# Round 0 of the experts by blocks of 128 tokens, head by head, and x moved in 16 outer pieces

## The chip, the cores and the metric

One core of a Trainium2 chip runs the whole program as one kernel. Its engines are TensorE (PE, with weight loads as PEld), VectorE (DVE), ScalarE (ACT) and GpSimd (POOL); SyncE (SP) issues the DMAs. They run side by side and wait for one another through semaphores. The metric is the device time in microseconds (us) of one execution; each number below is the median of several.

## The reference

x is 16 sequences of 256 tokens with 512 features. Four steps follow one another, each added to x with a gain: a retention layer and a feed-forward layer (here: attention), a long convolution over key, value and query, and a mixture of experts. The changed stage does the last two:

```python
x = x + jnp.tanh(g_xattn[1]) * _L1_xattn_ref(ctx_2048, ctx_2048, _layernorm(x, axis=-1), L1_xattn_ssm_kernel, L1_xattn_D, 8)
x = x + jnp.tanh(g_ffn[1]) * _L1_ffn_ref(_layernorm(x, axis=-1), L1_ffn_Wg, L1_ffn_bg, L1_ffn_Wgate, L1_ffn_bgate, ...)
```

The convolution forms products of key and value, convolves them along the feature axis with a Toeplitz matrix and adds a skip term, then weighs the result with the query. The experts are a router (softmax over six), six routed experts of 256 hidden features and a shared one of 512: `silu(gate) * up`, then `down`.

## The kernel before

Three blocks of code run one after the other: `scores_block`, `attn_block` and `experts_block`. A block ends when every engine and the DMAs it waits for are done. All orders are written out by hand, one list of calls for each engine; a list is executed strictly in order, and each call first waits on its semaphores.

**Attention to experts.** `attn_block` works on 8 chunks (NCH) of 512 tokens, each of 4 blocks (TJ) of 128. `store` (L708) writes each finished block of x to DRAM. `fetch_x` and `copy_x` (L693 to L706) bring the rows that round 0 of the experts needs into SBUF ahead of time; copy_x takes rows of the last chunk straight from SBUF. SP's last instruction of the block waits for all these DMAs (`early_in`).

**Which tokens a round has.** `experts_block` also has 8 rounds of 512 tokens: round q takes 32 tokens of each of the 16 sequences, 4 heads (CHD) of 8 tokens (CD). `row_block` (L3092) gives the rows of block j of a round in DRAM; it is used for loads (`load_x`, L1251) and for the stores of the result (`store`, L1281). Its outermost axis has 4 pieces of 32 rows.

**Convolution of a round.** Queries: `norm_x` (ACT), `turn_q` (PE transposes), `read_q` (ACT copies into `qe`). Keys and values are cut into 16 units u, four for each head hh = u // 4, with feature block lb = u % 4. For a unit POOL multiplies pairs (`pairs`, L1444 and L1447), ACT rounds them (`cut_kv`, L1794), POOL (in round 0) or DVE (later) takes the rest (L1452 or L2218), PE multiplies with the Toeplitz matrix (`unit`, 6 (lb + 1) matmuls of 288 columns), DVE multiplies with the queries (`multiply`, L2238 to L2242) and sums (`add_terms`, L2253). In round 0 POOL does the sums of units 2, 6, 9 and 13 (L1461 to L1465). Then `turn_x3` (PE, L2818), `add_x3` and `nat_stats` (DVE, L2260 to L2272), `nat_pow` (POOL), `nat_shift` (DVE, L2278), `norm_nat` (ACT, L1803), `turn_xn` (PE, L2829), `cut_xn` (ACT L1811, DVE L2283), each for two halves of the round.

**Experts of a round.** 16 tiles s: `gate` and `up` on PE (results in the banks ps_g and ps_u), `silu` on ACT, `weigh` on POOL, `gated` on DVE (L2181), `cut_hd`, `down`. `up` of tile s + 1 waits for `gated` of tile s. The convolution of round i + 1 is woven into the experts of round i; only round 0 has nothing beside it. There `logits` (L2839), the first step of the router, is the first matmul that needs the turned and normed rows.

## Time and profile before

| | us |
|---|---|
| median of 3 runs | 2033.63 (2032.94 to 2035.59) |
| profiled execution | 2035.08 |
| its span | 2033.3 |
| PE busy | 1907.3 |
| PE weight loads busy | 1550.1 |
| DVE busy | 1492.6 |
| POOL busy | 1024.6 |
| ACT busy | 993.7 |

The mean granted clock of PE is 0.974 of full. Attention ends at about 650 us, round 0 of the experts has its first logits matmul at 749.9, and the seven further rounds follow at intervals of about 164 us. Times in rows are us from the start of the span; an engine's idle time counts only where what it does next is waited for. A timeline row has start, duration, engine, line, operation and out<-in, then the idle time ahead of it and what ended it. A row that begins with a stretch (a:b) has its length, the busy time and count of PE, PEld, DVE, ACT and POOL, the granted clock (1 is full), the DMA share and GB/s. A wait has its sum, count and mean; an issue has ns of issuing (minimum, median, maximum).

### The profile page before, as it was taken

The page shows a single profiled execution, that of the slowest core. Times are in us where ns is not written, and L with a number is a line of the kernel's source. Part 1 is how long each engine was busy: PE and PEld are TensorE (multiplying, and loading weights), DVE is VectorE, ACT ScalarE, POOL GpSimd, SP SyncE. Part 2 cuts the span into 40 slices and gives each one's busy share as a digit, 9 for nine tenths or more (in the row PEclk, how much of TensorE's full clock was granted, in tenths as well). Part 3 has the DMA queues.
Part 4 walks back from the last instruction along what each step waited for, and adds up shares of the span by engine and source line. Part 5 has one row for each costly group of instructions (what it writes and reads, how often), then busy time and mean ns, then how long its engine had stood idle before and what let it go on. Part 6 is the DMA issues. An engine that isn't in the chain of part 4 may idle for free.

```text
span 2033.3 us, 27275 instructions
## 1 busy us (share of the span) xinstructions
PE 1907.3 (94%) x9892; PEld 1550.1 (76%) x9922; DVE 1492.6 (73%) x2233; ACT 993.7 (49%) x1420; POOL 1024.6 (50%) x790
## 2 busy tenths in 40 slices
PE   6999769999996669999999999999999999999997
PEld 5888756666652648888888887887887888888786
DVE  5877569888884867867876877876886886787422
ACT  4447557776764434345336336436435533533532
POOL 1110145444430856655655755756566665666454
PEclk9999889999999779999999999999999999999999
DMA  5866415566655203224234233342342432422431
GB/s 195 313 241 230 177 47 135 152 160 170 145 116 127 84 12 134 89 97 142 72 110 146 78 114 93 116 119 82 111 129 63 151 90 87 148 71 73 139 99 53
DMA packets 170113, 249.70 MB, mean 123 GB/s; under 512 B 91356, under 2 KB 92764, under 8 KB 163708
## 3 DMA queue, kind: packets, MB, share of 16 engines
q1 hardware_dynamic: 169692, 247.86, 39.7%
q8 instruction: 80, 1.31, 0.3%
q14 instruction: 53, 0.43, 0.1%
q10 hardware_dynamic: 288, 0.10, 0.0%
HBM read 193.13 MB, written 33.69 MB: 112 GB/s over the span
## 4 chain that ended last, share of the span: by engine, by line
PE 58%; DVE 4%; POOL 2%; issue 2%; ACT 1%; DMA 1%; ACTq 0%; POOLq 0%; DVEq 0%
PE e_ps_out L54 5%; PE e_ps_out L56 5%; PE e_ps_out L55 5%; PE e_ps_u L54 5%; PE e_ps_u L56 5%; PE e_ps_u L55 5%; PE e_ps_g L54 4%; PE e_ps_g L55 4%; PE e_ps_g L56 4%; PE e_ps_m L56 4%; PE e_ps_m L55 4%; PE e_ps_m L54 4%; DVE e_pstats L2266 1%; PE e_ps_m L2829 1%; PE e_ps_m L2784 1%
## 5 line engine op out<-in xcount | busy, mean ns | idle before, releaser
L1423 POOL TENSOR_TENSOR e_gu_lo<-e_gu_raw,e_gu_hi 128x1024 fp32r<-128x1024 f32 (+1 forms) x128 | 278.3, 2177 | 163.7 <-ACT e_gu_hi L1729 163.3
L2253 DVE TENSOR_REDUCE e_x3T<-e_zp 128x128 f32<-128x1024 f32 x124 | 257.4, 2076 | 1.2
L1428 POOL TENSOR_TENSOR e_dn_lo<-e_dn_raw,e_dn_hi 128x512 fp32r<-128x512 f32 x128 | 181.2, 1418 | 140.7 <-ACT e_dn_hi L1735 139.8
L54 PE MATMUL e_ps_u<-e_xn_hi,e_gu_hi 128*128 128x512 f32 x512 | 203.1, 397 | 8.4 <-DVE gate_held L2181 8.4
L2186 DVE TENSOR_TENSOR e_hd_lo<-gate_held,e_hd_hi 128x512 fp32r<-128x512 f32 x128 | 149.3, 1166 | 77.0 <-ACT e_hd_hi L1759 76.7
L54 PE MATMUL e_ps_out<-e_dn_hi,e_hd_hi 128*128 128x512 f32 x512 | 201.7, 394 | 0.0
L55 PE MATMUL e_ps_u<-e_xn_lo,e_gu_hi 128*128 128x512 f32 x512 | 199.9, 390 | 0.0
L56 PE MATMUL e_ps_u<-e_xn_hi,e_gu_lo 128*128 128x512 f32 x512 | 199.9, 390 | 0.0
L56 PE MATMUL e_ps_out<-e_dn_hi,e_hd_lo 128*128 128x512 f32 x512 | 199.5, 390 | 0.0
L55 PE MATMUL e_ps_out<-e_dn_lo,e_hd_hi 128*128 128x512 f32 x512 | 199.5, 390 | 0.0
L1435 POOL TENSOR_TENSOR gate_held<-e_sg,e_wb 128x512 f32<-128x512 f32 x96 | 136.3, 1420 | 109.7 <-ACT e_sg L1743 64.4
L1444 POOL TENSOR_TENSOR e_kv_raw<-e_ke 128x512 f32<-128x512 f32 x128 | 147.6, 1153 | 57.4 <-DVE e_kv_lo L2218 51.7
L54 PE MATMUL e_ps_m<-e_kv_hi,e_t_hi 128*128 128x288 f32 x574 | 169.6, 295 | 3.7 <-ACT e_qe L1773 3.7
L1794 ACT ACTIVATE e_kv_hi<-e_kv_raw 128x576 fp32r<-128x576 f32 x122 | 81.7, 676 | 184.4 <-POOL e_kv_raw L1447 97.2
L55 PE MATMUL e_ps_m<-e_kv_lo,e_t_hi 128*128 128x288 f32 x574 | 169.5, 295 | 0.0
L56 PE MATMUL e_ps_m<-e_kv_hi,e_t_lo 128*128 128x288 f32 x574 | 169.4, 295 | 0.0
L1729 ACT ACTIVATE e_gu_hi<-e_gu_raw 128x1024 fp32r<-128x1024 f32 (+1 forms) x128 | 120.6, 943 | 82.3 <-DMA e_gu_raw<-in_mgu 34.7
L2238 DVE TENSOR_TENSOR e_zp<-e_ps_m,e_qe 128x512 f32<-128x512 f32 x116 | 79.8, 688 | 106.3 <-PE e_ps_m L56 105.7
L1735 ACT ACTIVATE e_dn_hi<-e_dn_raw 128x512 fp32r<-128x512 f32 x128 | 79.2, 624 | 158.2 <-PE e_ps_out L56 105.0
L54 PE MATMUL e_ps_g<-e_xn_hi,e_gu_hi 128*128 128x512 f32 x384 | 149.8, 390 | 1.7 <-POOL e_gu_lo L1423 1.7
L55 PE MATMUL e_ps_g<-e_xn_lo,e_gu_hi 128*128 128x512 f32 x384 | 149.8, 390 | 0.0
L56 PE MATMUL e_ps_g<-e_xn_hi,e_gu_lo 128*128 128x512 f32 x384 | 149.6, 390 | 0.0
(321 smaller groups left out, 5003.5 us busy)
## 6 DMA issues: line engine op xcount, KB each, us to landing
e_gu_raw<-in_mgu SPq DMA_DIRECT2D x96, 512.0 KB, 3.8
e_dn_raw<-in_md SPq DMA_DIRECT2D x128, 256.0 KB, 3.3
e_wb<-wts SPq DMA_DIRECT2D x8, 1536.0 KB, 6.6
c<-in_ctxT SPq DMA_DIRECT2D x8, 1024.0 KB, 6.6
raw_w<-in_w1T SPq DMA_DIRECT2D x8, 1024.0 KB, 4.9
x_held<-in_w2T SPq DMA_DIRECT2D x8, 1024.0 KB, 7.4
gates<-gate_held SPq DMA_DIRECT2D x8, 1024.0 KB, 5.0
vals<-o SPq DMA_DIRECT2D x8, 1024.0 KB, 5.1
```

The costliest lines, as they stand in the source:

```text
L54: nc.tensor.matmul(out, w_hi, x_hi, start=first, stop=False, skip_group_check=skip)
L55: nc.tensor.matmul(out, w_hi, x_lo, start=False, stop=False, skip_group_check=skip)
L56: return nc.tensor.matmul(out, w_lo, x_hi, start=False, stop=last, skip_group_check=skip)
L1423: nc.gpsimd.tensor_tensor(gu_lo[:, s % 2, a], gu_raw[:, s % 2, a], f32(gu_hi[:, s % 2, a]), ALU.subtract).then_inc(gulo_done, 1)
L1428: nc.gpsimd.tensor_tensor(dn_lo[:, s % 2], dn_raw[:, s % 2], f32(dn_hi[:, s % 2]), ALU.subtract).then_inc(dnlo_done, 1)
L1435: nc.gpsimd.tensor_tensor(sgw[:], sg[:], wb[:, (s - SHARED) // 2], ALU.mult).then_inc(sgw_done, 1)
L1444: nc.gpsimd.tensor_tensor(out[:, :, 0:32].rearrange("p b (d i) -> p b d i", i=CD), view(ke, m * B * EXT, (EXT, B), (0, 4), (1, CD)), view( ...
L1729: nc.scalar.activation(gu_hi[:, s % 2, a], gu_raw[:, s % 2, a], ACT.Copy).then_inc(guhi_done, 1)
L1794: nc.scalar.activation(pair_slot(q, hh, u % KT, False), kv_raw[:, u % 2], ACT.Copy).then_inc(kvhi_done, 1)
L2186: nc.vector.tensor_tensor(hd_lo[:, s % 2], hd[:], f32(hd_hi[:, s % 2]), ALU.subtract).then_inc(hdlo_done, 1)
L2238: nc.vector.tensor_tensor(zv(68, (21, 4), (1, 8)), yv(0, (8, 4), (1, 8)), qv(0, (1, 4), (1, 8)), ALU.mult).then_inc(prod_done, 1)
L2253: nc.vector.tensor_reduce(x3T[:, lb].rearrange("p (b n) -> p b n", b=B)[:, :, hh * CD:(hh + 1) * CD], zv(5, (1, 8), (21, 8)), AX.X, ALU.ad ...
```

## The change

1. `row_block` has 16 outer pieces (one for each sequence) of 8 rows; block j of a round now is head j of all sequences. `qe` and `x3T` are laid out to match.
2. `fetch_x` runs one turn of the loop earlier and fetches 12 of the 16 pieces of each block; `fetch_late_x` and `copy_x` bring the rest. The small constants come along in the attention.
3. Round 0 turns, reads, adds and norms the four blocks one by one (`first_...`), in the banks ps_g and ps_u, woven into the 16 units. Two cuts (units 0 and 1) go from POOL to DVE. Pairs of odd heads lie in gu_hi and gu_lo instead of xn_hi and xn_lo.
4. In rounds 1 to 6, both `turn_x3` of the next round stand earlier on PE, and add_x3 and nat_stats of the second half earlier on DVE.

```diff
+            sp.dma_start(rest[:, 3, 0:32], dram["skipD"]).then_inc(early_in, 16)
+            sp.dma_start(rest[:, 3, 32:64], dram["wroute"].rearrange("p k e -> p (k e)")).then_inc(early_in, 16)
...
         def fetch_x():
             sp.wait_ge(oT_done, 4 * NCH)
             sp.wait_ge(x2_out, START + 16 * TJ * (NCH - 2))
-            for j in range(TJ - 1):
-                sp.dma_start(early(keep)[0][:, j], row_block(dram["x2"], 0, j)).then_inc(early_in, 16)
+            for j in range(TJ):
+                sp.dma_start(early(keep)[0][0:CD * (B - 4), j], row_block(dram["x2"], 0, j)[0:B - 4]).then_inc(early_in, 16)
+        def fetch_late_x():
             sp.wait_ge(x2_out, START + 16 * TJ * (NCH - 1))
-            for b in range(2):
-                sp.dma_start(early(keep)[0][32 * b:32 * b + 32, TJ - 1], row_block(dram["x2"], 0, TJ - 1)[b]).then_inc(early_in, 16)
+            for j in range(TJ):
+                sp.dma_start(early(keep)[0][CD * (B - 4):CD * (B - 2), j], row_block(dram["x2"], 0, j)[B - 4:B - 2]).then_inc(early_in, 16)
         def copy_x(j):
-            b = 2 + j // 2
+            b = B - 2 + j // 2
             sp.wait_ge(x2_done, START + 4 * (NCH - 1) + j + 1)
-            sp.dma_start(early(keep)[0][32 * b:32 * b + 32, TJ - 1], x2[0:32, j]).then_inc(early_in, 16)
+            for hh in range(TJ):
+                sp.dma_start(early(keep)[0][CD * b:CD * (b + 1), hh], x2[CD * hh:CD * (hh + 1), j]).then_inc(early_in, 16)
...
+            if i == NCH + 1:
+                fetch_late_x()
             at(turn_h, i - 2, 2)
             at(turn_h, i - 2, 3)
-            if i == NCH + 1:
+            if i == NCH:
                 fetch_x()
             if i == NCH + 1:
                 copy_x(0)
+                copy_x(2)
...
         if q == 0 and hh % 2 == 1 and m < 3:
-            t = (xn_lo if low else xn_hi)[:].rearrange("p k n -> p (k n)")
+            t = (gu_lo if low else gu_hi)[:].rearrange("p s a k n -> p (s a k n)")
...
+    def turns(q):
+        return 2 * q + (2 if q > 0 else 0)
+    def bank(n):
+        return (ps_g, ps_u)[n % 2][:]
...
-        conv_pow(0)
-        pairs(0, 0)
-        pairs(0, 1)
-        cut_kv(0, 0)
-        cut_kv(0, 1)
         pairs(0, 2)
+        first_pow(1)
         pairs(0, 3)
         cut_kv(0, 2)
         cut_kv(0, 3)
@@ -1495,35 +1518,37 @@
         pairs(0, 5)
         cut_kv(0, 4)
         cut_kv(0, 5)
+        add_terms(0, 2)
         pairs(0, 6)
         pairs(0, 7)
         cut_kv(0, 6)
-        add_terms(0, 2)
         cut_kv(0, 7)
         pairs(0, 8)
+        first_nat_pow(0)
         pairs(0, 9)
         cut_kv(0, 8)
+        add_terms(0, 6)
         cut_kv(0, 9)
         pairs(0, 10)
         pairs(0, 11)
         cut_kv(0, 10)
-        add_terms(0, 6)
         cut_kv(0, 11)
         pairs(0, 12)
+        add_terms(0, 9)
+        first_nat_pow(1)
         pairs(0, 13)
         cut_kv(0, 12)
         cut_kv(0, 13)
         pairs(0, 14)
-        add_terms(0, 9)
+        pairs(0, 15)
         cut_kv(0, 14)
-        pairs(0, 15)
         cut_kv(0, 15)
         add_terms(0, 13)
...
+            if n < 2:
+                act.wait_ge(unit_done, START + CHD * KT)
...
+        def first_read_q(j):
+            act.wait_ge(q_filled, START + j + 1)
+            out = qe[:].rearrange("p (k j b) e -> p k j b e", k=KT, j=TJ)[:, :, j]
+            src = bank(j).rearrange("p (k b i) -> p k b i", k=KT, i=CD)
+            nc.scalar.activation(out[:, :, :, 0:CD], src, ACT.Copy).then_inc(qe_done, 1)
+            nc.scalar.activation(out[:, :, :, CD:EXT], src[:, :, :, 0:EXT - CD], ACT.Copy).then_inc(qe_done, 1)
...
+        keys(0, 0)
+        cut_t(0, 0)
+        first_norm_x(0)
+        cut_kv(0, 0)
+        first_read_q(0)
+        cut_kv(0, 1)
+        for j in range(1, TJ):
+            first_norm_x(j)
         setup()
-        cut_t(0, 0)
-        norm_x(0)
-        keys(0, 0)
-        read_q(0, 0)
-        cut_kv(0, 0)
+        first_read_q(1)
+        cut_kv(0, 2)
         cut_t(0, 1)
-        cut_kv(0, 1)
-        read_q(0, 1)
-        cut_dn(0, 0)
-        cut_kv(0, 2)
+        first_read_q(2)
         cut_kv(0, 3)
+        first_read_q(3)
         keys(0, 1)
         for u in range(4, 7):
             cut_kv(0, u)
         cut_t(0, 2)
         keys(0, 2)
-        for u in range(7, 11):
-            cut_kv(0, u)
-        cut_gu(0, 0)
-        cut_gu(0, 1)
+        cut_dn(0, 0)
+        cut_kv(0, 7)
+        cut_kv(0, 8)
+        first_norm_nat(0)
+        cut_kv(0, 9)
+        cut_kv(0, 10)
+        first_cut_xn(0)
         cut_kv(0, 11)
         keys(0, 3)
         cut_t(0, 3)
-        for u in range(12, 16):
-            cut_kv(0, u)
+        cut_kv(0, 12)
+        first_norm_nat(1)
+        cut_kv(0, 13)
+        cut_kv(0, 14)
+        first_cut_xn(1)
+        cut_kv(0, 15)
+        cut_dn(0, 1)
         keys(1, 0)
         cut_kv(1, 0)
-        cut_dn(0, 1)
-        norm_nat(0, 0)
-        norm_nat(0, 1)
-        cut_xn(0, 0)
-        cut_xn(0, 1)
+        first_norm_nat(2)
+        cut_gu(0, 0)
+        first_cut_xn(2)
+        cut_gu(0, 1)
+        first_norm_nat(3)
+        first_cut_xn(3)
...
+            if q == 0 and lb == 0:
+                dve.wait_ge(qe_done, START + 2 * hh + 2)
+            elif u == 0:
+                dve.wait_ge(qe_done, START + 8 + 4 * q)
...
+        def first_add_x3(j):
+            dve.wait_ge(nat_filled, j + 1)
+            row = rows_of(0)[:, j]
+            nc.vector.scalar_tensor_tensor(out=row, in0=bank(0), scalar=keep["gains"][:, 1:2], in1=row, op0=ALU.mult,
+                                           op1=ALU.add).then_inc(x3_done, 1)
...
-        norm_stats(0)
         add_skip(0, 0)
-        norm_shift(0)
+        first_stats(0)
+        first_stats(1)
+        first_shift(0)
         cut_t(0, 0)
+        cut_kv(0, 0)
+        first_stats(2)
+        first_stats(3)
+        first_shift(1)
+        cut_kv(0, 1)
         add_skip(0, 1)
+        multiply(0, 0)
+        cut_t(0, 1)
         setup()
-        cut_t(0, 1)
-        multiply(0, 0)
-        add_skip(0, 2)
         add_terms(0, 0)
         multiply(0, 1)
         multiply(0, 2)
         add_terms(0, 1)
+        add_skip(0, 2)
         multiply(0, 3)
         add_terms(0, 3)
         multiply(0, 4)
         add_terms(0, 4)
         cut_t(0, 2)
+        first_add_x3(0)
+        first_nat_stats(0)
         multiply(0, 5)
         multiply(0, 6)
         add_terms(0, 5)
+        first_nat_shift(0)
         multiply(0, 7)
         add_terms(0, 7)
         add_skip(0, 3)
         multiply(0, 8)
+        first_cut_xn(0)
+        add_terms(0, 8)
         cut_t(0, 3)
-        add_terms(0, 8)
+        first_add_x3(1)
+        first_nat_stats(1)
         multiply(0, 9)
         multiply(0, 10)
         add_terms(0, 10)
+        first_nat_shift(1)
         multiply(0, 11)
         add_terms(0, 11)
         multiply(0, 12)
         multiply(0, 13)
+        first_cut_xn(1)
         add_terms(0, 12)
+        first_add_x3(2)
+        first_nat_stats(2)
         multiply(0, 14)
         add_terms(0, 14)
+        first_nat_shift(2)
         multiply(0, 15)
         add_terms(0, 15)
-        add_x3(0, 0)
-        nat_stats(0, 0)
-        add_x3(0, 1)
-        nat_stats(0, 1)
-        nat_shift(0, 0)
-        nat_shift(0, 1)
+        first_cut_xn(2)
+        first_add_x3(3)
+        first_nat_stats(3)
+        first_nat_shift(3)
         norm_stats(1)
-        cut_xn(0, 0)
-        cut_xn(0, 1)
+        first_cut_xn(3)
...
             at(cut_hd, i, 12)
+            at(add_x3, i + 1, 1)
+            at(nat_stats, i + 1, 1)
+            at(gated, i, 13)
             at(nat_shift, i + 1, 0)
-            at(gated, i, 13)
             at(cut_t, i + 2, 0)
             at(cut_hd, i, 13)
-            at(add_x3, i + 1, 1)
-            at(nat_stats, i + 1, 1)
+            at(nat_shift, i + 1, 1)
             at(gated, i, 14)
...
+        def first_turn_q(j):
+            pe.wait_ge(xq_done, START + j + 1)
+            if j >= 2:
+                pe.wait_ge(qe_done, START + 2 * j - 2)
+            for k in range(KT):
+                last = nc.tensor.transpose(bank(j)[:, k * P:(k + 1) * P], xq[:, j, k * P:(k + 1) * P], ident[:])
+            last.then_inc(q_filled, 1)
...
+        def first_turn_x3(j):
+            pe.wait_ge(red_done, START + sums(KT * (j + 1)))
+            pe.wait_ge(pool_step, SETUP + 3 * sum(u < KT * (j + 1) for u in SPLIT))
+            if j == 0:
+                pe.wait_ge(qe_done, START + 6)
+            else:
+                pe.wait_ge(x3_done, START + j)
+            for k in range(KT):
+                last = nc.tensor.transpose(bank(0)[:, k * P:(k + 1) * P], x3T[:, k, j * P:(j + 1) * P], ident[:])
+            last.then_inc(nat_filled, 1)
...
-        turn_q(0, 0)
-        turn_q(0, 1)
-        for u in range(16):
-            unit(0, u)
-        turn_x3(0, 0)
-        turn_x3(0, 1)
-        turn_xn(0, 0)
-        turn_xn(0, 1)
+        first_turn_q(0)
+        unit(0, 0)
+        unit(0, 1)
+        first_turn_q(1)
+        unit(0, 2)
+        first_turn_q(2)
+        unit(0, 3)
+        first_turn_q(3)
+        unit(0, 4)
+        unit(0, 5)
+        unit(0, 6)
+        first_turn_x3(0)
+        unit(0, 7)
+        unit(0, 8)
+        first_turn_xn(0)
+        unit(0, 9)
+        unit(0, 10)
+        first_turn_x3(1)
+        unit(0, 11)
+        unit(0, 12)
+        unit(0, 13)
+        first_turn_xn(1)
+        unit(0, 14)
+        first_turn_x3(2)
+        unit(0, 15)
+        first_turn_xn(2)
+        first_turn_x3(3)
+        first_turn_xn(3)
...
             at(down, i, 11)
+            at(turn_x3, i + 1, 0)
             at(gate, i, 13)
-            at(turn_x3, i + 1, 0)
+            at(turn_x3, i + 1, 1)
             at(up, i, 13)
             at(gate, i, 14)
             at(down, i, 12)
-            at(turn_x3, i + 1, 1)
...
-    return rows.rearrange("(j b g r) d -> g j b r d", j=TJ, b=4, g=NCH)[q, j]
+    return rows.rearrange("(b g j r) d -> g j b r d", b=B, g=NCH, j=TJ)[q, j]
```

**SP, end of the attention block.** x is DRAM, o the rows of round 0, x_held the last chunk in SBUF. Before:

```order
L673 DMA_TRANSPOSE ayqT<-ayq 128x8x128
L710 DMA x<-x_held 128x512 x3
L679 DMA_TRANSPOSE ahqT<-ahq 128x16x128 x4
L697 DMA o<-x 128x1x512 x3
L700 DMA o<-x 32x512 x2
L706 DMA o<-x_held 32x512
L710 DMA x<-x_held 128x512 x2
L706 DMA o<-x_held 32x512
L710 DMA x<-x_held 128x512 x2
```

After:

```order
L699 DMA o<-x 96x1x512 x4
L715 DMA x<-x_held 128x512
L673 DMA_TRANSPOSE ayqT<-ayq 128x8x128
L715 DMA x<-x_held 128x512 x3
L679 DMA_TRANSPOSE ahqT<-ahq 128x16x128 x2
L704 DMA o<-x 16x1x512 x4
L679 DMA_TRANSPOSE ahqT<-ahq 128x16x128 x2
L711 DMA o<-x_held 8x512 x8
L715 DMA x<-x_held 128x512 x4
```

The large loads of x now stand ahead of the last chunk's turns, and all copies ahead of the last four stores.

**ACT, start of round 0.** e_ke are keys, e_xq normed queries, e_qe their turned copies, e_kv_hi the rounded pairs. Before, and then after, from the constants (e_bd, e_wr) on. Before:

```order
L1837 ACTIVATE e_bd<-gate_held 96x512
L1838 ACTIVATE e_wr<-e_xnat 128x4x8
L1787 ACTIVATE e_t_hi<-gate_held 128x512
L1765 ACTIVATE e_xq<-o,e_shift,e_rstd 128x512 x4
L1780 ACTIVATE e_ke<-stage 128x64x8
L1781 ACTIVATE e_ke<-stage 128x64x4
L1772 ACTIVATE e_qe<-e_ps_out 128x128x8
L1773 ACTIVATE e_qe<-e_ps_out 128x128x4
L1794 ACTIVATE e_kv_hi<-e_kv_raw 128x576
L1787 ACTIVATE e_hd_hi<-gate_held 128x512
L1794 ACTIVATE e_kv_hi<-e_kv_raw 128x576
```

After:

```order
L1881 ACTIVATE e_bd<-gate_held 96x512
L1882 ACTIVATE e_wr<-gate_held 128x4x8
L1796 ACTIVATE e_qe<-e_ps_u 128x4x16x8
L1797 ACTIVATE e_qe<-e_ps_u 128x4x16x4
L1841 ACTIVATE e_kv_hi<-e_kv_raw 128x576
L1834 ACTIVATE e_hd_hi<-gate_held 128x512
L1796 ACTIVATE e_qe<-e_ps_g 128x4x16x8
L1797 ACTIVATE e_qe<-e_ps_g 128x4x16x4
L1841 ACTIVATE e_kv_hi<-e_kv_raw 128x576
L1796 ACTIVATE e_qe<-e_ps_u 128x4x16x8
L1797 ACTIVATE e_qe<-e_ps_u 128x4x16x4
L1827 ACTIVATE e_ke<-stage 128x64x8
```

Ahead of this piece of after stand the keys of head 0, query block 0 with its read and the cuts of units 0 and 1. The cuts of units 2 and 3 (L1841) now stand behind the reads of query blocks 1 and 2, and the keys of head 1 (last row) behind the read of block 3.

**DVE, end of the round that is woven into round 1.** e_ps_m holds turned x3, gate_held<-e_ps_u is `gated`, e_pshift is `nat_shift`. Before:

```order
L2260 SCALAR_TENSOR_TENSOR x_held<-e_ps_m,gains,x_held 128x1024
L2266 BN_STATS e_pstats<-x_held 128x6 x2
L2269 BN_AGGR e_pmv<-e_pstats 128x2 x2
L2272 TENSOR_SCALAR e_pve<-e_pmv 128x2
L2186 TENSOR_TENSOR e_hd_lo<-gate_held,e_hd_hi 128x512
L2278 SCALAR_TENSOR_TENSOR e_pshift<-e_pmv,e_prstd 128x2
L2181 SCALAR_TENSOR_TENSOR gate_held<-e_ps_u,vecs,gate_held 128x512
L2214 TENSOR_TENSOR e_t_lo<-gate_held,e_t_hi 128x512
L2186 TENSOR_TENSOR e_hd_lo<-gate_held,e_hd_hi 128x512
L2260 SCALAR_TENSOR_TENSOR x_held<-e_ps_m,gains,x_held 128x1024
L2266 BN_STATS e_pstats<-x_held 128x6 x2
```

After:

```order
L2360 SCALAR_TENSOR_TENSOR x_held<-e_ps_m,gains,x_held 128x1024
L2366 BN_STATS e_pstats<-x_held 128x6 x2
L2369 BN_AGGR e_pmv<-e_pstats 128x2 x2
L2372 TENSOR_SCALAR e_pve<-e_pmv 128x2
L2242 TENSOR_TENSOR e_hd_lo<-gate_held,e_hd_hi 128x512
L2360 SCALAR_TENSOR_TENSOR x_held<-e_ps_m,gains,x_held 128x1024
L2366 BN_STATS e_pstats<-x_held 128x6 x2
L2369 BN_AGGR e_pmv<-e_pstats 128x2 x2
L2372 TENSOR_SCALAR e_pve<-e_pmv 128x2
L2237 SCALAR_TENSOR_TENSOR gate_held<-e_ps_u,vecs,gate_held 128x512
L2378 SCALAR_TENSOR_TENSOR e_pshift<-e_pmv,e_prstd 128x2
```

The second add and its statistics now stand ahead of `gated` of tile 13.

## Rows read from the trace of the kernel before

**Rows 1.** The page, busy us (share) xinstructions of each engine, whole span
```profile
PE 1907.3 (94%) x9892; PEld 1550.1 (76%) x9922; DVE 1492.6 (73%) x2233; ACT 993.7 (49%) x1420; POOL 1024.6 (50%) x790
```

**Rows 2.** End of the span: SP's timeline, stretch, SP's wait, landings of 256 KB stores
```profile
2018.93 3.15 SPq L1284 DMA_DIRECT2D out<-e_x_next  x4
2021.00:2032.00 11.00, 0.00 (x0) 0.00 (x0) 0.00 (x0) 0.00 (x0) 0.00 (x0) 0.67 0.25 91
SPq L3084 <- DMA out<-e_x_next: 10.8, 1, 10.8
DMA to landing us min/median/max: 2.3/2.9/8.3
```

**Rows 3.** Attention to experts: timeline by engine, issues of L697, SP's wait
```profile
640.77 3.13 PEld L1072 LDWEIGHTS ps_y<-w2q,ahqT 128*128 128x128 bf16 x16 [1.34 <-DVE x_held L974]
L697 SPq DMA_DIRECT2D o<-x x3: 511/537/950, 643.8 to 645.4; - x3
649.93 0.75 DVE L974 SCALAR_TENSOR_TENSOR x_held<-ps_y,adq,ax 128x512 f32<-128x512 f32 x1 [4.74 <-PE ps_y L1072]
SPq L1104 <- DMA o<-x_held: 6.8, 1, 6.8
658.57 0.34 SPq L1248 DMA_DIRECT2D e_skip<-in_skipD  x1
```

**Rows 4.** Rounds 1 to 5, the timeline of one; last row: PE's waits, 800 to 2033
```profile
1040.64 2.11 DVE L2253 TENSOR_REDUCE e_x3T<-e_zp 128x128 f32<-128x1024 f32 x1
1043.93 0.39 PE L54 MATMUL e_ps_g<-e_xn_hi,e_gu_hi 128*128 128x512 f32 x1
1047.73 1.28 DVE L2260 SCALAR_TENSOR_TENSOR x_held<-e_ps_m,gains,x_held 128x1024 f32<-128x1024 f32 x1 [4.98 <-PE e_ps_m L2818]
1052.00 2.34 DVE L2278 SCALAR_TENSOR_TENSOR e_pshift<-e_pmv,e_prstd 128x2 f32<-128x2 f32 x1 [0.59 <-POOL e_prstd L1475]
1063.86 0.16 DVE L2278 SCALAR_TENSOR_TENSOR e_pshift<-e_pmv,e_prstd 128x2 f32<-128x2 f32 x1
1063.88 0.47 PE L54 MATMUL e_ps_u<-e_xn_hi,e_gu_hi 128*128 128x512 f32 x1 [1.68 <-DVE gate_held L2181]
PE e_ps_u L54 <- DVE gate_held L2181: 8.4, 5, 1.7
```

**Rows 5.** Round 0, POOL and DVE: timeline, one stretch, and POOL's waits in it
```profile
667.59 1.40 POOL L1444 TENSOR_TENSOR e_kv_raw<-e_ke 128x512 f32<-128x512 f32 x1 [4.06 <-ACT e_ke L1781]
679.05 1.04 POOL L1444 TENSOR_TENSOR e_kv_raw<-e_ke 128x512 f32<-128x512 f32 x1
686.47 1.98 DVE L2253 TENSOR_REDUCE e_x3T<-e_zp 128x128 f32<-128x1024 f32 x1
686.94 1.41 POOL L1452 TENSOR_TENSOR e_xn_lo<-e_kv_raw,e_xn_hi 128x576 fp32r<-128x576 f32 x1
688.31 2.14 POOL L1461 TENSOR_TENSOR e_wb<-e_wb 128x512 f32<-128x512 f32 x1
664.00:732.00 68.00, 44.96 (x256) 41.05 (x256) 56.67 (x85) 24.86 (x42) 62.54 (x65) 0.83 0.19 65
POOL e_kv_lo L1452 <- ACT e_kv_hi L1794: 0.8, 1, 0.8
```

**Rows 6.** Round 0: matmuls at two clocks, ACT's read; DVE's multiplies, grouped (660 to 732)
```profile
673.66 0.44 PE L54 MATMUL e_ps_m<-e_kv_hi,e_t_hi 128*128 128x288 f32 x1
680.19 0.29 PE L54 MATMUL e_ps_m<-e_kv_hi,e_t_hi 128*128 128x288 f32 x1
667.46 1.02 ACT L1772 ACTIVATE e_qe<-e_ps_out 128x1024 f32<-128x1024 f32 x1
L2238 DVE TENSOR_TENSOR e_zp<-e_ps_out,e_qe 128x512 f32<-128x512 f32 x8 | 5.5, 686 | 3.5 <-PE e_ps_out L56 3.4
```

**Rows 7.** Round 0, its end: POOL's last sum and the first logits matmul
```profile
727.33 0.45 POOL L1465 TENSOR_TENSOR e_x3T<-e_wb 128x128 f32<-128x128 f32 x1
749.86 0.59 PE L2839 MATMUL e_ps_g<-e_xn_hi,e_wr 128*16 128x512 f32 x1 [2.42 <-issue]
```

163 lines of the change are left out of this document (107 added, 56 removed).

## Prediction

> **What bounds the kernel now.** I read the page first: TensorE (PE) is busy 94% of the span [rows 1], so only stretches in which PE stands still or runs slow can give time back. The 40 slices and a table of stretches show three of them. (a) After the last result: the last store is issued by 2022.1 us, the span ends at 2033.3, and in between the core's 16 DMA engines are busy a quarter of the time, no engine computes, and SyncE waits 10.8 us for the stores [rows 1, 2]. (b) Between attention and experts: DVE's last instruction ends at 650.7, the first one of the experts stands at 658.6, and SyncE waits 6.8 us for a copy of x [rows 3]. (c) Round 0 of the experts, 664 to 750 us: PE is busy 45 of 68 us at a granted clock of 0.83 while GpSimd (POOL) is busy 62.5 of 68 and DVE 56.7 [rows 5]; POOL sets the pace, DVE is close behind. Behind that PE is dense; its only repeated gap is one of 1.68 us a round, five in all [rows 4].
>
> **Term 1, the last stores: -8.6 us.** A quarter of 16 engines is four, and `row_block` had an outermost axis of four pieces. 4 x 256 KB at about 91 to 100 GB/s take the 10.8 us that SyncE waits. The stores of x2 in the attention, also 256 KB each, whose outermost axis is the 128 partitions, land 2.9 us after their issue in the median [rows 2]. With 16 pieces I expect the same of the stores. The last issue begins about 1.0 us before 2022.1 and lands at about 2024.0; with the 0.4 to 0.8 us of ending behind it the span closes at about 2024.7, 8.6 earlier. Bounds: the fastest such landing in the attention tail (2.3) gives -9.2, the slowest (8.3) -3.2.
>
> The Trainium skill, "DMA: Bandwidth & Descriptors", section "Why a DMA increments its semaphore by 16 and not by 1", says that a DMA issued by SyncE uses the largest count up to 16 that divides the slowest axis of both sides. By it the old pieces use four engines, as the share of 0.25 shows, and the new ones sixteen; it gives the term above, and if it didn't hold the term would be zero (a rival below).
>
> **Term 2, the boundary: -6.8 us.** `fetch_x` now runs one turn earlier, at about 614, with 12 pieces; the rest is four small loads and eight copies of 8 rows. The last ones wait for block 2 of the last chunk, which DVE finishes at 645.2. SyncE needs 0.51 to 0.95 us for an issue of this kind; the four copies of block 0 are out by then, and four copies and three stores more take it to about 649.5, and store 3, which needs DVE's end at 650.7, is its last work at 651.2. The copies, 16 KB each, have landed by then (2.3 to 2.9 us of landing from 648), and the block ends at about 651.6 instead of 658.4 [rows 2, 3]. Queued behind the added issues are SyncE's turns of y and h. Four issues (2.2 us) now stand before the turn of y, which waits for DVE anyway. Four small loads stand before the turn of block 2's h; its matmuls wait for DVE at 640.78, not for it [rows 3], which is the cover. Cover gone: up to +2.
>
> **Term 3, the moved turns: -8.7 us.** In rounds 1 to 5 PE waits 1.68 us before `up` of tile 15, for `gated` of tile 14. DVE is late because add_x3 and the statistics of the second half stand in front, and DVE before that had idled 4.98 us for the first turn [rows 4]. After the change the first turn stands before `gate` 13 (its last reduce ends at 1042.75, PE is free at 1043.93: 1.2 us of margin, 0.6 in the tightest round), the second before `up` 13. DVE then does both halves by about 1051.3, and `gated` 14 follows `up` 14 at about 1059.4 instead of 1063.0; `up` 15 can start at 1062.05. The turns themselves cost what they did. The added order has one new link: nat_shift of half 1 now stands before gated 14 and waits for POOL's pow behind weigh 14. I put that at 58.2, 1.1 us before `up` 14 ends. Five times 1.67 and 0.36 of the last round: 8.7. If the new turn misses its reduce or nat_shift comes late, a round gives less: bound -4.
>
> **Term 4, round 0: +13.5 us.** I walked the new order with durations of [rows 5 to 7]; times are from the start of the experts' block. Units: POOL's pairs 1.32 (1.04 and a small piece), its cut 1.40, its add_terms 3.85 (2.14 and two smaller steps); DVE's multiply 1.6 (five pieces, the largest 0.69), reduce 2.0; a turn of four 0.8 to 1.0; a unit of PE 6(b+1) matmuls for block b, at 0.24 us each while the clock is at half and 0.13 at full. ACT's read of one block is an estimate, 1.0 us, from half the 1.02 and 0.59 of the old reads plus their starts.
> - POOL's first pair starts at 2.0 instead of 9.2, since `keys` no longer stands behind the constants, the norm and its four activations. Two cuts (2.8) go to DVE.
> - But cut_kv 2 of ACT now stands behind read_q 1, that behind PE's turn 1, that behind unit 1, and that behind DVE's cut of unit 1, which waits for pow 1 and shift 1. I get: DVE's cut of unit 1 at 11.7, unit 1 to 14.6, turn 15.6, read 16.6, ACT's cut 17.2, POOL's cut 2 at 18.7. The same ring turns again for unit 2 (22.2), turn 2, read 2, POOL's cut 3 at 26.0, and for unit 3 (30.7), turn 3, read 3, keys 1 at 33.4. Only then can POOL start pairs 4. Before, pairs 4 start at 20.7: +12.7, the 7.2 and the 2.8 included.
> - From pairs 4 to the end of add_terms 13 POOL took 48.7. It gets three more pows (2.1), and it now waits for DVE: for the statistics of block 0 (2.5; DVE stood still before, from 41 to 49, since first_add_x3(0) stands ahead of multiply 5 and 6 and needs unit 6) and for multiply 9 (4.1), where DVE carries 2.6 us of norm work a block inside the phase. Less other small shifts: 57.0, +8.3.
> - The tail. Before, 22.1 us from that point to the first logits matmul, nearly all of it a chain of single operations [rows 7]. Now only block 3 is left, but two reduces stand between: 14.6, -7.5.
> Sum: 12.7 + 8.3 - 7.5 = +13.5; the first logits come at 105 instead of 91.5 after the block's start, and by the clock of the trace at 756.6 instead of 749.9. Bounds: with PE at its full level in the three rings -4.0, and if the waits of POOL for DVE are half as long -3.3; with shifts that wait for POOL each time +6. So +6 to +20.
>
> A rule speaks against this part. The rows show it first: a shift of 128x2 takes 0.16 us at 1063.86 and 2.34 at 1052.00, while POOL computes [rows 4]. The Trainium skill, "SBUF — State Buffer", section "Who interferes with whom", says that a DVE instruction with two SBUF inputs and a GpSimd instruction that reads SBUF exclude each other for its whole length. The new round has eight such DVE instructions beside POOL's work (two cuts, six shifts).
>
> From the rows alone I count one POOL instruction of about 1.2 us for the first shift and one more later, both in the walk; the full price is the last rival.
>
> **Sum:** +13.5 - 6.8 - 8.7 - 8.6 = -10.6 us. The profiled execution took 2035.08 (span 2033.3 and 1.8 around it), 1.4 over the median of 2033.63; the terms are differences and I take them off the median: **2023.0 us**.
>
> **Rivals.**
> - The rings don't bite (PE at full clock, reads and turns early): POOL would work from 2.0 on without waits, 60.2 (667.6 to 727.8) - 2.8 + 2.1 = 59.5 us, and 14.6 of tail: logits at 76, 15.4 earlier than before in place of 13.5 later. In full that is 1994; halfway from the forecast 2009. For it speaks that POOL was never idle over 0.8 us in the old round [rows 5]; against it that the waits stand in the code in this order. 10%.
> - The stores stay on four engines: term 1 is lost, 2031.6. For it: no row shows 16 pieces. Against: other 256 KB moves. 4%.
> - A new wait takes the place of the 1.68 us (turn of half 0 before its reduce, nat_shift behind POOL): term 3 is lost, 2031.7. Against: the margins above. 5%.
> - Slower: DVE and POOL exclude each other. If each of the eight added two-input instructions takes 2.34 us as the slow shift did [rows 4], 18.7 instead of the 2.4 counted, and all of it lies on the path, round 0 costs +29.8 and the whole takes 2039.3. It decides only when all eight pay. 4%.
>
> **Chances.** Forecast 77%; the rivals 10, 4, 5 and 4. A difference of 0.2% (4.1 us) is about what a measurement of this kernel can tell from none: faster below 2029.6, slower above 2037.7. The first rival and nearly all of the forecast are faster: 0.87. The two lost terms are within it: 0.09. Slower: 0.04. The favourable bounds together give 2015, and I go on to 2012 for rings that bite less than that. The unfavourable ones all at once would be over 2040; round 0 at +20 and an uncovered boundary give 2031.5, and the two lost terms lie there too: 2012 to 2032 leaves out the first rival and the last.
>
> **What would show it.** Stores: the wait of SyncE at the end under 4 us, with the DMA share well over 0.25. Boundary: no wait for a DMA there, 7 us less between DVE's last residual and the first expert instruction. Turns: no wait of `up` 15 for gated in rounds 1 to 5. Round 0: POOL idle behind ACT's cuts before pairs 4, which start 31 to 35 us after the block's start, and the logits at 100 to 111 us. I am wrong if POOL's pairs 4 come before 25, if the logits come before 91, or if PE has a new gap per round.

## The result

The changed kernel takes **2023.26 us** (median of four executions, 2020.17 to 2025.24), the kernel before 2033.35 (2032.94 to 2035.59). The ratio is 0.9947, 95% interval 0.9930 to 0.9964: faster by 0.5%, 10.1 us. The forecast was 2023.0. Its sum came out almost to the digit, but two of its four terms were too small by some 2 us each in opposite directions, and one effect was not in it at all. Two executions of the experiments below, one of store_old with 4954.76 us and one of act_only with 3898.76 us, belong to a slow state and are in none of the figures.

The profiled execution has a span of 2020.3 us, 13.0 less than that of before. Cut at four marks that both traces have, the difference splits like this:

| stretch | before | after | difference | forecast |
|---|---|---|---|---|
| start to the first DMA issue of the experts | 658.57 | 650.83 | -7.7 | -6.8 |
| from there to the first logits (round 0) | 91.3 | 107.3 | +16.0 | +13.5 |
| first to last logits (seven rounds) | 1146.65 | 1136.15 | -10.5 | -8.7 |
| last logits to VectorE's end | 124.4 | 122.4 | -2.0 | 0 |
| VectorE's end to the end of the span | 12.4 | 3.6 | -8.7 | -8.6 |
| sum | | | -13.0 | -10.6 |

The medians differ by 10.1, not 13.0, because the profiled execution of before was 1.7 over its median and that of after 1.1 under it.

**The end of the span**, after. SyncE's timeline, its wait and a stretch of 3 us, as in [rows 2] (columns of the stretch: its length, busy PE, PEld, DVE, ACT and POOL, granted clock, DMA share, GB/s).

Timeline, changed kernel:

```profile
2014.67 2.58 SPq L1298 DMA_DIRECT2D out<-e_x_next  x4
```

Waits (us in total, times, longest), changed kernel:

```profile
SPq L3245 <- DMA out<-e_x_next: 2.7, 1, 2.7
```

A stretch, changed kernel:

```profile
2017.00:2020.00 3.00, 0.00 (x0) 0.00 (x0) 0.00 (x0) 0.00 (x0) 0.00 (x0) 0.79 0.75 255
```

The wait of 10.8 us is 2.7, and the DMA engines that were a quarter busy at 91 GB/s are three quarters busy at 255 GB/s.

**The boundary**, after: TensorE's row for the third block of the last chunk, SyncE's copies, VectorE's last residual and the first issue of the experts, as in [rows 3].

```profile
640.76 3.61 PE L1078 MATMUL ps_y<-w2q,ahqT 128*128 128x512 bf16 x16 [2.18 <-DMA ahqT<-ahq]
642.48 5.61 SPq L711 DMA_DIRECT2D o<-x_held  x8
648.88 0.75 DVE L980 SCALAR_TENSOR_TENSOR x_held<-ps_y,adq,ax 128x512 f32<-128x512 f32 x1 [3.72 <-PE ps_y L1078]
650.83 0.34 SPq L1263 DMA_DIRECT2D e_skip<-in_skipD  x1
```

No wait for a DMA stands at the end of the block any more. SyncE issues copies and stores until VectorE's last store can go.

**The rounds**, after. `gated` of tile 14 delays no `up`: TensorE has no wait at all from 780 us to its end, where [rows 4] have five of 1.7. Two first logits rows, one round apart, of before and of after:

```profile
1243.88 0.40 PE L2839 MATMUL e_ps_g<-e_xn_hi,e_wr 128*16 128x512 f32 x1
1407.63 0.40 PE L2839 MATMUL e_ps_g<-e_xn_hi,e_wr 128*16 128x512 f32 x1
```

```profile
1247.95 0.40 PE L2980 MATMUL e_ps_g<-e_xn_hi,e_wr 128*16 128x512 f32 x1
1409.53 0.40 PE L2980 MATMUL e_ps_g<-e_xn_hi,e_wr 128*16 128x512 f32 x1
```

163.75 us a round before, 161.58 after (in the other stalled rounds 163.5).

**Round 0**, after: GpSimd's timeline, and the first logits of TensorE, as in [rows 5, 7]. The block starts at 650.8.

```profile
666.57 1.40 POOL L1466 TENSOR_TENSOR e_kv_lo<-e_kv_raw,e_kv_hi 128x576 fp32r<-128x576 f32 x1 [4.25 <-ACT e_kv_hi L1841]
675.12 1.41 POOL L1466 TENSOR_TENSOR e_kv_lo<-e_kv_raw,e_kv_hi 128x576 fp32r<-128x576 f32 x1 [7.15 <-ACT e_kv_hi L1841]
683.80 1.04 POOL L1458 TENSOR_TENSOR e_kv_raw<-e_ke 128x512 f32<-128x512 f32 x1 [7.27 <-ACT e_ke L1828]
703.89 0.56 POOL L1490 TENSOR_TENSOR e_prstd<-e_pve,e_mhalf 128x1 f32<-128x1 f32 x1 [3.57 <-DVE e_pve L2342]
725.22 2.00 POOL L1475 TENSOR_TENSOR e_wb<-e_wb 128x512 f32<-128x512 f32 x1 [5.98 <-DVE e_wb L2315]
742.84 0.46 POOL L1479 TENSOR_TENSOR e_x3T<-e_wb 128x128 f32<-128x128 f32 x1
758.12 0.59 PE L2980 MATMUL e_ps_g<-e_xn_hi,e_wr 128*16 128x512 f32 x1 [1.68 <-issue]
```

GpSimd waits 4.3, 7.2 and 7.3 us, three times in a row, for ScalarE. In the old round, once its pairs were under way, its longest wait for ScalarE was 0.8 [rows 5]. Pairs 4 start 33.0 us after the block's start, where it was 20.5.

### The profile page after: what moved, and what is told of

It is laid out like the page before. It is cut to its first block, busy times and chain, and to the rows that moved or that the text cites. A ratio compares the mean times of both kernels' runs of the same rounds, so it can differ in the third digit from the quotient of the medians.

```text
span 2020.3 us, 27306 instructions
## 1 busy us (share of the span) xinstructions
PE 1908.6 (94%) x9892; PEld 1553.9 (77%) x9922; DVE 1487.2 (74%) x2247; ACT 994.1 (49%) x1426; POOL 1021.3 (51%) x791
## 4 chain that ended last, share of the span: by engine, by line
PE 63%; POOL 2%; issue 1%; DVE 1%; ACT 0%; DVEq 0%; POOLq 0%; ACTq 0%
PE e_ps_out L54 6%; PE e_ps_out L56 6%; PE e_ps_out L55 6%; PE e_ps_u L54 6%; PE e_ps_u L55 6%; PE e_ps_u L56 6%; PE e_ps_g L55 4%; PE e_ps_g L56 4%; PE e_ps_g L54 4%; PE e_ps_m L54 4%; PE e_ps_m L56 4%; PE e_ps_m L55 4%; PE e_ps_m L2898 1%; PE e_ps_m L2970 1%; PE e_ps_m L2959 1%
## 5 line engine op out<-in xcount | busy, mean ns | idle before, releaser
L1841 ACT ACTIVATE e_kv_hi<-e_kv_raw 128x576 fp32r<-128x576 f32 x122 | 81.7, 676 | 170.4 <-PE e_ps_m L56 86.7
```

Of the source, the lines that this page charges most:

```text
L1841: nc.scalar.activation(pair_slot(q, hh, u % KT, False), kv_raw[:, u % 2], ACT.Copy).then_inc(kvhi_done, 1)
```

## Experiments

Twelve kernels ran, in three groups of four, each group on one chip together with the kernel before (medians 2032.9, 2033.3 and 2033.3). "Start" is the first DMA issue of the experts' block, "round 0" the time from there to the first logits, both in the profiled execution.

| kernel | median | ratio, 95% interval | start | round 0 |
|---|---|---|---|---|
| before | 2033.35 | 1 | 658.57 | 91.3 |
| changed, first group | 2024.23 | 0.9954 (0.9941 to 0.9966) | 653.12 | 107.2 |
| store4 | 2024.07 | 0.9953 (0.9941 to 0.9965) | 650.99 | 105.8 |
| late_fetch | 2027.52 | 0.9970 (0.9960 to 0.9980) | 658.96 | 106.1 |
| loose | 2006.96 | 0.9873 (0.9860 to 0.9887) | 652.90 | 89.8 |
| turns_only | 2026.88 | 0.9964 (0.9953 to 0.9976) | 657.45 | 91.3 |
| store4x4 | 2033.30 | 0.9996 (0.9988 to 1.0005) | 651.76 | 105.7 |
| slot | 2022.03 | 0.9936 (0.9924 to 0.9948) | 652.81 | 105.8 |
| loose2 | 2003.81 | 0.9853 (0.9840 to 0.9866) | 650.61 | 88.3 |
| store_old | 2036.26 | 1.0010 (1.0001 to 1.0019) | 654.02 | 106.9 |
| act_only | 2009.60 | 0.9883 (0.9868 to 0.9898) | 650.57 | 94.0 |
| cuts_pool | 2005.24 | 0.9865 (0.9850 to 0.9880) | 651.90 | 88.3 |
| best | 2003.94 | 0.9856 (0.9842 to 0.9869) | 650.81 | 87.1 |

### Do sixteen outer pieces make the stores fast?

The theory: the outermost axis of the address pattern sets how many of the 16 DMA engines a store uses. The rival: something else in the new layout does, and the term is luck. There are three attempts; the third is the one that tells them apart.

**store4**, the same bytes and places written as 4 x 4 pieces:

```diff
-                sp.dma_start(row_block(dram["out"], g, j), rows_of(g)[:, j]).then_inc(y_out, 16)
+                sp.dma_start(row_block(dram["out"], g, j).rearrange("(a b) r d -> a b r d", a=4), rows_of(g)[:, j]).then_inc(y_out, 16)
```

> The changed kernel, with only the address pattern of its stores written as 4 x 4 pieces of 8 rows (outermost axis 4) in place of 16 x 8 rows. The bytes and places are the same. Theory (the outermost axis sets how many of the 16 DMA engines a store uses): SyncE's wait at the end goes from 2.7 back to about 10.8 us with a DMA share of 0.25 there, the kernel gets 8 to 9 us slower than the changed one, and as a second effect the load of the last round that landed 6.6 us after its issue in the kernel before is late again, another 1.7. Rival: the two outer axes are merged before the DMA is built, or the count of engines is set by the whole number of rows; then nothing changes, within 2 us.

This is the rival's outcome: 2024.07 beside 2024.23 of the changed kernel in the same group, and SyncE's wait at the end is 2.7 as in the changed kernel. Two axes whose steps fit together seem to count as one, so this kernel says nothing on the theory. It serves as a second copy of the changed one.

**store4x4**, four DMAs of 64 KB for each block:

```diff
-                sp.dma_start(row_block(dram["out"], g, j), rows_of(g)[:, j]).then_inc(y_out, 16)
+                for a in range(0, B, 4):
+                    sp.dma_start(row_block(dram["out"], g, j)[a:a + 4], rows_of(g)[CD * a:CD * (a + 4), j]).then_inc(y_out, 16)
```

> The changed kernel, with each store of a block of the result issued as four DMAs of four outer pieces (32 partitions, 64 KB) in place of one of 16 pieces. The pattern of 4 x 4 x 8 rows in one DMA was as fast as 16 x 8, so the two axes count as one; here the outermost axis cannot be more than four. Theory (the outermost axis sets how many DMA engines a store uses, always the same ones): SyncE's wait at the end is 8 to 11 us again with a DMA share of about 0.25, the kernel gets 7 to 12 us slower than the changed one (2 of it for 12 more issues), and the load of the last round is late again. Rival (each DMA takes other engines, or the bytes of a DMA decide): the wait at the end stays under 5 us and the kernel is 0 to 3 us slower.

The time went up as forecast, to 2033.30. But the rows do not show the cause. Here are SyncE's timeline at the end and a stretch of it:

Timeline, store4x4:

```profile
2017.48 10.54 SPq L1299 DMA_DIRECT2D out<-e_x_next  x16
```

A stretch, store4x4:

```profile
2018.00:2029.00 11.00, 0.70 (x4) 0.24 (x2) 1.49 (x3) 0.00 (x0) 0.00 (x0) 0.64 0.24 90
```

Waits (us in total, times, longest), store4x4:

```profile
SPq L3246 <- DMA out<-e_x_next: 2.0, 1, 2.0
```

The share of 0.24 fits the theory, yet the 16 issues take 10.5 us by themselves at 0.66 each, and SyncE waits only 2.0 us behind them. With four DMA engines or with sixteen, this kernel would have ended about there. It loses 7.3 us behind VectorE's end and 3.7 in the last round, where a load is late again (see store_old).

**store_old** is the changed kernel whose stores alone use the pattern of before. Its rows are written to the places of other tokens, so its output is a permutation of the right one; computation, bytes and issues are the same.

```diff
-                sp.dma_start(row_block(dram["out"], g, j), rows_of(g)[:, j]).then_inc(y_out, 16)
+                sp.dma_start(dram["out"].rearrange("(j b g r) d -> g j b r d", j=TJ, b=4, g=NCH)[g, j], rows_of(g)[:, j]).then_inc(y_out, 16)
```

> The changed kernel, with only its stores of the result written with the address pattern of the kernel before (four pieces of 32 rows, one DMA of 256 KB a block). The same bytes go out in as many DMAs, but the rows of a round land at the places of other tokens, so the output is permuted. Four DMAs in place of one couldn't tell this, since 16 issues at 0.65 us alone fill the 10.5 us at the end. Theory (the outermost axis sets how many DMA engines a store uses): SyncE's wait at the end is 10 to 11 us, DMA share 0.25 there, and TensorE waits 1.7 to 1.9 us for GpSimd in the last round again, since a load is late behind the stores: 9 to 11 us slower than the changed kernel. Rival for the last: that wait hangs on the time of the round and not on the stores, and only 8 to 9 us come.

Below are SyncE's timeline and wait at the end, TensorE's only wait behind 780 us, a stretch of the end and one behind TensorE's wait, and ScalarE's row for a weight load in the last round:

Timeline, store_old:

```profile
2021.77 3.12 SPq L1298 DMA_DIRECT2D out<-e_x_next  x4
```

Waits (us in total, times, longest), store_old:

```profile
SPq L3245 <- DMA out<-e_x_next: 10.8, 1, 10.8
PE e_ps_g L54 <- POOL e_gu_lo L1437: 2.5, 1, 2.5
```

Two stretches, store_old:

```profile
2022.00:2033.00 11.00, 0.99 (x5) 0.49 (x3) 1.78 (x3) 0.00 (x0) 0.00 (x0) 0.78 0.23 77
1925.00:1929.00 4.00, 4.00 (x11) 3.16 (x12) 0.49 (x1) 0.71 (x1) 1.86 (x2) 0.59 0.76 305
```

Timeline, store_old:

```profile
1920.14 0.63 ACT L1762 ACTIVATE e_dn_hi<-e_dn_raw 128x512 fp32r<-128x512 f32 x1 [5.13 <-DMA e_dn_raw<-in_md]
```

Four issues take 3.1 us, and the wait is 10.8 again with a share of 0.23: the theory's outcome. In the trace's DMA records four packets, at times three or five, are in flight at every moment from 2025 to 2031. What the run doesn't separate is the number of outer pieces from their size, for four pieces hold 64 KB each where sixteen hold 16, and their places in DRAM differ too.

The ratio goes from 0.9954 (first group) to 1.0010 (third group, another chip): 0.56%, 11.4 us, more than the 8.7 at the end. The rest lies in the last round. A weight load issued there at 1912.7, behind 1 MB of stores, lands more than 7 us later; ScalarE waits 5.1 us for it, and TensorE 2.5 us for what follows. Behind that wait TensorE's granted clock is 0.59 for some 4 us. From the last logits to VectorE's end store_old takes 126.9 us, the changed kernel 122.4. The kernel before has this wait too:

Waits (us in total, times, longest), kernel before:

```profile
PE e_ps_g L54 <- POOL e_gu_lo L1423: 1.7, 1, 1.7
```

Timeline, kernel before:

```profile
1918.89 0.63 ACT L1735 ACTIVATE e_dn_hi<-e_dn_raw 128x512 fp32r<-128x512 f32 x1 [4.29 <-DMA e_dn_raw<-in_md]
```

There the clock stays at 1.00 behind it, and the stretch takes 124.4 us. In the changed kernel the load issued at 1910.07 has landed by 1912.26. The slow stores did not only end late, they stood in front of loads. This is the -2.0 that the forecast lacked; in store_old, where the clock fell as well, the same thing costs 4.5 us.

### Which part of the rounds' gain is the moved turns?

**turns_only** is the kernel before with the steady loop's part of point 4 of the change. The order of the round that is woven into round 1 is written out apart, and was left as it was:

```diff
             at(cut_hd, i, 12)
+            at(add_x3, i + 1, 1)
+            at(nat_stats, i + 1, 1)
+            at(gated, i, 13)
             at(nat_shift, i + 1, 0)
-            at(gated, i, 13)
             at(cut_t, i + 2, 0)
             at(cut_hd, i, 13)
-            at(add_x3, i + 1, 1)
-            at(nat_stats, i + 1, 1)
-            at(gated, i, 14)
             at(nat_shift, i + 1, 1)
+            at(gated, i, 14)
...
+            at(turn_x3, i + 1, 0)
             at(gate, i, 13)
-            at(turn_x3, i + 1, 0)
+            at(turn_x3, i + 1, 1)
             at(up, i, 13)
             at(gate, i, 14)
             at(down, i, 12)
-            at(turn_x3, i + 1, 1)
```

> The kernel before, with nothing but part 4 of the change: in rounds 1 to 6 both turns of x3 earlier on TensorE, and the second add, its statistics and its shift earlier on VectorE. Theory (term 3): the 1.7 us wait of `up` 15 goes in each of five rounds; start to start a round takes 161.6 in place of 163.5 us, as in the changed kernel, and the kernel gets 8.7 to 10 us faster than before. If the prediction's size is right and not the trace's, 8.7. The wait of 1.7 us for GpSimd in the last round belongs to the stores by theory and stays; by the rival it belonged to the timing of the rounds and goes too. Rival: rounds get shorter in the changed kernel because its loads and stores have 16 pieces; then only a part comes.

TensorE's waits from 780 us on:

```profile
PE e_ps_u L54 <- DVE gate_held L2181: 1.7, 1, 1.7
PE e_ps_g L54 <- POOL e_gu_lo L1423: 1.9, 1, 1.9
```

One wait for `gated` is left of five, in the one round that kept its order. That round takes 163.51 us from logits to logits, the five behind it 161.58 to 161.69: both orders in one execution, 1.9 us apart. From the first to the last logits the seven rounds take 9.0 us less than before. In span the kernel gains 8.4, in medians 6.4 (0.9964, interval 4.9 to 9.6 us), less than the 8.7 to 10 expected. The wait for GpSimd in the last round stays, 1.9 us, as the store theory says: it is not a matter of the rounds' timing. Behind it the granted clock is 0.57 from 1914 to 1918, where it stayed at 1.00 in the kernel before, and the stretch from the last logits to VectorE's end is 1.7 us longer (126.2 against 124.4). That takes back a part of what the rounds gave, in the profiled execution at least.

### What is the boundary worth?

**late_fetch** puts the fetch back to its old place in the loop, still with 16 pieces:

```diff
-            if i == NCH + 1:
-                fetch_late_x()
             at(turn_h, i - 2, 2)
             at(turn_h, i - 2, 3)
-            if i == NCH:
-                fetch_x()
             if i == NCH + 1:
+                fetch_x()
+                fetch_late_x()
                 copy_x(0)
-                copy_x(2)
             at(store, i - 2, 0)
             at(turn_y, i - 1, 1)
             at(store, i - 2, 1)
+            if i == NCH + 1:
+                copy_x(2)
```

> The changed kernel with the fetch of x for round 0 back in the last turn of the attention's loop, and the second group of copies behind two of the last stores, as before the change. Theory of term 2: SyncE waits for a DMA at the end of the attention again, the first instruction of the experts comes 6 to 8 us later than the 650.8 of the changed kernel, and the whole gets 6 to 8 us slower. Rival: the 16-piece pattern alone made the fetch quick (16 DMA engines in place of fewer); then the boundary stays within 2 us of the changed kernel's.

Timeline, late_fetch:

```profile
644.22 3.58 SPq L699 DMA_DIRECT2D o<-x  x4
654.18 2.65 SPq L711 DMA_DIRECT2D o<-x_held  x4
```

Waits (us in total, times, longest), late_fetch:

```profile
SPq L1109 <- DMA o<-x_held: 0.4, 1, 0.4
```

Timeline, late_fetch:

```profile
658.96 0.34 SPq L1262 DMA_DIRECT2D e_skip<-in_skipD  x1
```

The block starts at 658.96 again, 5.8 to 8.1 us later than in profiles of the changed kernel. But SyncE no longer waits for a DMA: only 0.4 us in place of 6.8. It is busy issuing from 644.2 to 657.8, with 16 small DMAs in place of 7. So the fetch at its old place costs what the theory says, but by its issues and not by a wait for landing.

That wait went with the old pieces, which the prediction did not see; the rival of this run had it right for the wait, and wrong for the start. In the kernel before, while SyncE waits for the loads and copies of x:

```profile
655.00:658.00 3.00, 0.00 (x0) 0.00 (x0) 0.00 (x0) 0.00 (x0) 0.00 (x0) 0.50 0.26 100
```

This is about the share and the rate of the last stores in [rows 2], and the DMA records again have four packets in flight: the three large loads of x used the pattern with four outer pieces too. With 16 pieces the late place costs its issues instead; the old pieces at the earlier place were not run.

In medians only 3.3 us come (2027.52 against 2024.23), not the 6 to 8 expected. The profiled execution is the slowest of nine, 1.6 over their median, and the changed kernel's own start moves by 2.3 us between profiles, as the next one shows.

**slot** is about that difference. Profiles of the changed kernel differ at 641 us. Shown are TensorE's row for the third block, and the stretch 641 to 644, in the first group's copy (compare 640.76 above).

Timeline, changed kernel, first group:

```profile
641.40 5.30 PE L1078 MATMUL ps_y<-w2q,ahqT 128*128 128x512 bf16 x16 [2.12 <-DMA ahqT<-ahq]
```

A stretch, changed kernel, first group:

```profile
641.00:644.00 3.00, 2.60 (x7) 0.98 (x8) 0.20 (x1) 0.00 (x0) 0.00 (x0) 0.62 0.59 111
```

A stretch, changed kernel:

```profile
641.00:644.00 3.00, 3.00 (x16) 1.34 (x14) 0.00 (x0) 0.00 (x0) 0.00 (x0) 1.00 0.86 160
```

After an idle time of 2.1 us (2.2 in the other) the granted clock is 0.62 in one execution and 1.00 in another, and the 16 matmuls take 5.3 in place of 3.6 us. It is so in three of the nine profiles with this order (this one, loose, store_old), and in none of before, turns_only, late_fetch, slot and best. TensorE idles there for the turn of h that SyncE issues, which now stands behind the four late loads. slot moves these to an earlier place:

```diff
-            if i == NCH + 1:
-                fetch_late_x()
             at(turn_h, i - 2, 2)
...
             at(turn_h, i - 1, 0)
+            if i == NCH:
+                fetch_late_x()
```

> The changed kernel itself, run again beside the three that follow, so that each is compared with it on the same chip. Its first four executions spread from 2020.2 to 2025.2, wider than those of the kernel before. Expected: ratio to the kernel before 0.993 to 0.996. If the spread comes from round 0 (the time at which TensorE's clock rises there), its logits come at a different time in another profile; if it comes from the rest, they come at 107 us after the block's start again.

> The changed kernel with the four late loads of x issued one turn of the loop earlier, in a gap of SyncE (between its turns of h for blocks 0 and 1 of the last chunk), in place of ahead of the turn for block 2. In the changed kernel that turn comes 2.6 us later; TensorE idles 2.2 us there at 640.8, and in the profiles with a time near 2024 its clock is at half for some 3 us behind this idle time, in those near 2020 it is not. Theory: without that idle time the half clock does not come, all executions fall at 2018 to 2021, and the median is 3 to 5 us below the changed kernel's. Rival: the half clock comes from something else, and the executions still fall in two groups near 2020 and 2024.

The changed kernel's own second set of executions (median 2024.23) lies at 2020.5 once and at 2024.0 to 2024.5 four times, the one with the clock at half among the latter. Round 0 took 107.2 and 107.3 in its two profiles, but 105.8 in that of store4, the other copy, whose profiled execution took 2020.27. There the granted clock is 0.65 from 10 to 15 us after the block's start, where the two others have 0.50. So both places vary: between the profiles at 2024.23 and 2020.27 the start differs by 2.1 us and round 0 by 1.4.

slot's median is 2022.03 (0.9936, against 0.9954, the intervals overlap), not the 3 to 5 us of the theory. Its clock is at 1.00 at 641 us, and yet its executions run from 2018.0 to 2022.1, and the profiled one, at the upper end, starts the experts at 652.81. VectorE's last residual stands at 650.58 there, against 648.88 and 651.21 in the changed kernel, since TensorE now waits 1.9 us for the turn of the fourth block. So half the clock explains 1.7 us of a late start in those executions that have it, and a later rise of the clock in round 0 goes with some 1.5 us more; what decides either stays open.

### Do the rings cost what the walk says?

**loose** cuts them: ScalarE no longer has work of GpSimd's chain behind a read, and TensorE turns blocks 2 and 3 one unit earlier.

```diff
         for j in range(1, TJ):
             first_norm_x(j)
+        cut_kv(0, 2)
+        cut_kv(0, 3)
+        keys(0, 1)
+        cut_t(0, 1)
         setup()
         first_read_q(1)
-        cut_kv(0, 2)
-        cut_t(0, 1)
         first_read_q(2)
-        cut_kv(0, 3)
         first_read_q(3)
-        keys(0, 1)
...
         first_turn_q(1)
+        first_turn_q(2)
         unit(0, 2)
-        first_turn_q(2)
-        unit(0, 3)
         first_turn_q(3)
+        unit(0, 3)
         unit(0, 4)
```

> The changed kernel with the rings of round 0 cut: ScalarE does its cuts of units 2 and 3 and the keys of head 1 ahead of the reads of query blocks 1 to 3, and TensorE turns query block 2 ahead of unit 2 and block 3 ahead of unit 3. Theory of term 4 (three rings through TensorE, ScalarE and GpSimd cost 12.7 us before pairs 4): pairs 4 start at about 16 us after the block's start in place of 33.1, and the logits come 8 to 15 us earlier than 107.3; the kernel gets 8 to 15 us faster. Rival 1: GpSimd's waits for VectorE (3.6 for the statistics of block 0, 6.0 for multiply 9) grow by what is won, since VectorE is the next bound; then pairs 4 are early but the logits gain under 5 us. Rival 2: the rings only covered work of GpSimd, and nothing changes.

GpSimd's pairs 4, and its two longest waits from 654 to 735:

Timeline, loose:

```profile
667.93 1.49 POOL L1458 TENSOR_TENSOR e_kv_raw<-e_ke 128x512 f32<-128x512 f32 x1
```

Waits (us in total, times, longest), loose:

```profile
POOL e_prstd L1490 <- DVE e_pve L2342: 3.6, 1, 3.6
POOL e_wb L1475 <- DVE e_wb L2315: 3.5, 1, 3.5
```

Pairs 4 start 15.0 us after the block's start in place of 33.0, and round 0 takes 89.8 in place of 107.2. The median is 2006.96, 17.3 us under the changed kernel on the same chip and more than the 8 to 15 expected. Of the 18.0 us of the rings 17.4 reach the logits; neither rival holds, for the waits for VectorE stay as they were (3.6) or shrink (6.0 to 3.5).

**act_only** has the first half of this diff alone, and TensorE's order is that of the changed kernel.

> The changed kernel with only ScalarE's half of the cut of the rings: its cuts of units 2 and 3 and the keys of head 1 stand ahead of the reads of query blocks 1 to 3; TensorE's order is the changed kernel's. With both halves pairs 4 started 15.1 us after the block's start, not at 33.1, and the kernel took 2007.0. Theory (the ring closes in ScalarE's order, where work of GpSimd's chain stands behind a read that it does not need): pairs 4 come at 15 to 16 us, and the time is 2006 to 2009. Rival (TensorE's turns behind the units matter as well): 2010 to 2016.

Timeline, act_only:

```profile
665.62 1.49 POOL L1458 TENSOR_TENSOR e_kv_raw<-e_ke 128x512 f32<-128x512 f32 x1
672.59 2.78 POOL L1466 TENSOR_TENSOR e_gu_lo<-e_kv_raw,e_gu_hi 128x576 fp32r<-128x576 f32 x2 [3.47 <-ACT e_gu_hi L1841]
```

Waits (us in total, times, longest), act_only:

```profile
POOL e_wb L1475 <- DVE e_wb L2315: 6.0, 1, 6.0
```

Pairs 4 come at 15.1 us here too, so the ring closed in ScalarE's list. The cut of unit 4 then waits 3.5 us for ScalarE, which now has all three reads in front and with them TensorE's turns behind units 2 and 3; round 0 takes 94.0 against 89.8. The time, 2009.60, lies between the theory's range (to 2009) and the rival's (from 2010). ScalarE's half is worth 13 of the 17 us in round 0, TensorE's the other 4.

**loose2** is loose with two more moves, against the two waits that are left:

```diff
         unit(0, 5)
-        unit(0, 6)
         first_turn_x3(0)
+        unit(0, 6)
...
         pairs(0, 12)
-        add_terms(0, 9)
-        first_nat_pow(1)
         pairs(0, 13)
         cut_kv(0, 12)
+        add_terms(0, 9)
+        first_nat_pow(1)
```

> The kernel with the rings cut (15.1 us to pairs 4, logits at 89.9 after the block's start), and two more moves: TensorE turns x3 of block 0 ahead of unit 6, not behind it, and GpSimd makes pairs 13 and the cut of unit 12 ahead of add_terms 9. They aim at its two waits for VectorE, 3.6 us (statistics of block 0) and 3.5 us (multiply 9). Theory (GpSimd and its waits still set the pace): logits 3 to 6 us earlier, the kernel at 2001 to 2004. Rival: VectorE, busy 77 of 90 us there, is the bound by now; the waits go and come back elsewhere, and the time changes by less than 2 us.

Waits from 652 to 730 (us in total, times, longest), loose2:

```profile
POOL e_prstd L1490 <- DVE e_pve L2342: 0.7, 1, 0.7
POOL e_wb L1475 <- DVE e_wb L2315: 3.4, 2, 2.5
```

A stretch, loose2:

```profile
665.00:735.00 70.00, 44.35 (x255) 40.56 (x253) 62.73 (x102) 20.68 (x39) 56.26 (x59) 0.79 0.18 57
```

The first wait fell from 3.6 to 0.7, the second stayed at 3.4 in two parts, and single waits for ScalarE grew to 1.5 and 1.7. Round 0 gives 1.5 us (88.3), not 3 to 6, and that is no more than it differs between profiles of one order (105.7 to 107.3 above). The median of 2003.81 is 3.2 under loose, on another chip and with intervals that just overlap; the block starts 2.3 us earlier in its profiled execution than in that of loose, which has the clock at half at 641 us. VectorE is busy 62.7 of 70 us and GpSimd 56.3. That speaks for the rival, but doesn't show it.

**cuts_pool** asks which of the two binds. It is loose2 with the cuts of units 0 and 1 back on GpSimd (the last two removals are in VectorE's list):

```diff
         nc.gpsimd.memset(w[:, :, 72], 1.0).then_inc(pool_step, 1)
+        cut_kv(0, 0)
         pairs(0, 2)
         first_pow(1)
+        cut_kv(0, 1)
         pairs(0, 3)
...
-        cut_kv(0, 0)
         first_stats(2)
         first_stats(3)
         first_shift(1)
-        cut_kv(0, 1)
```

> The kernel with the rings cut and its two further moves (2003.8), with the cuts of units 0 and 1 back on GpSimd. In that kernel VectorE is busy 62.7 of the 70 us from 665 to 735 and GpSimd 56.3. Theory A (VectorE is the bound of round 0 by now): moving 1.5 us off it costs nothing or gives up to 1.5 us. Theory B (GpSimd still sets the pace, as in the round before the change): 2.8 us more on GpSimd make it 1.5 to 3 us slower.

Round 0 takes 88.3 us as in loose2: 2.8 us more on GpSimd cost nothing in the one profile of each. The medians, 2005.24 and 2003.81, are 1.4 us apart, within their intervals. Theory B finds no support, though its lower end of 1.5 us is no more than round 0 varies by. That VectorE alone is the bound isn't shown either, since relieving it gave nothing.

**best** is loose2 with slot's move.

> The kernel with the rings cut and its two further moves (2003.8), with the four late loads of x in SyncE's gap one turn earlier as well (alone, that gave executions from 2018.0 to 2022.1, against 2020.2 to 2025.2 of the changed kernel). Theory: without the idle time of TensorE at 640.8 its clock is never at half there, and the median is 1 to 2 us below 2003.8. Rival: the end of the attention is as long as before the move, since the last turn of h then waits for VectorE's step for block 3 and not for SyncE, and the time stays within 1 us.

The median is 2003.94 (0.9856), beside 0.9853 of loose2: no difference. The clock at 641 us is 1.00 in both profiles. Round 0, whose order is that of loose2, takes 87.1 against 88.3. Either kernel is 1.4 to 1.5% faster than the one before and 1.0% faster than the changed one: a few moves in the order of round 0 brought about twice what the whole change did (19.5 us more, against 10.1).

## Why the prediction held, and where not

**Term 1, stores, -8.6.** Right in cause and size: -8.7 at the end of the span, and store_old gives it back. The share of 0.25 in [rows 2] was the right thing to read. The runs agree with the rule that the prediction cites from the Trainium skill ("DMA: Bandwidth & Descriptors", section "Why a DMA increments its semaphore by 16 and not by 1"): the share is 0.75 at 16 pieces and 0.23 at four. What the step missed: eight rounds store, not one. The stores of seven end beside other work, and behind one of these seven, in the last round, stood a load that was on the path: -2.0. The wait stood in a view that I had, with 1.7 us for GpSimd next to the five for VectorE; [rows 4] left it out.

**Term 2, boundary, -6.8.** The profiled execution gives -7.7, the other profile of the same kernel -5.4, the medians of late_fetch -3.3. The size was about right, the reason in part: the old wait of 6.8 us was one for loads of four pieces (share 0.26), so the cause of term 1 was at work here too, and late_fetch shows the wait gone with the fetch still late. The cover that the text named (TensorE waits for VectorE at 640.78, not for the turn of h) was gone: the row at 640.76 now waits 2.2 us for the DMA, and in some executions the clock falls to half behind it. The bound of +2 for that case was about right (1.7 measured).

**Term 3, turns, -8.7.** Right in cause; each of the five rounds gives 2.0 us in the mean (1.93 to 2.17), not 1.67. The step that was mis-sized took the idle time in the wait's row as the price. These are the rows around the stall of before:

```profile
1389.12 0.39 PE L56 MATMUL e_ps_g<-e_xn_hi,e_gu_lo 128*128 128x512 f32 x1
1391.17 0.47 PE L54 MATMUL e_ps_u<-e_xn_hi,e_gu_hi 128*128 128x512 f32 x1 [1.67 <-DVE gate_held L2181]
```

From start to start it is 2.05 us where two matmuls of this kind stand 0.23 apart: 1.82 lost. Rows of 0.39 us follow each other every 0.23, so idle time counted from the end of such a row misses 0.16. The matmul behind the stall is followed by the next after 0.31 (1391.48), not 0.23, which makes it 1.90. What is left is under 0.1 in four of the rounds, and 0.27 in the one shown, which stays unexplained. Five times 2.0 and some 0.5 in the first and last round are the 10.5. The new link (the second nat_shift behind GpSimd's pow) cost nothing.

**Term 4, round 0, +13.5.** +16.0. The walk to pairs 4 had the right steps, and two small errors in it cancelled: it started 1.7 us late, and its second ring was 1.3 us too short (7.3 from cut 2 to cut 3, measured 8.6). Times are from the start of the block:

| | forecast | after |
|---|---|---|
| end of VectorE's cut of unit 1 | 11.7 | 10.0 |
| end of unit 1 | 14.6 | 13.1 |
| end of GpSimd's cut 2 | 18.7 | 17.1 |
| end of GpSimd's cut 3 | 26.0 | 25.7 |
| start of pairs 4 | 33.4 | 33.0 |
| end of add_terms 13 | 90.4 | 92.5 |
| first logits | 105.0 | 107.3 |

The logits come 2.3 us late against the forecast, and one line of the sum holds more than that, GpSimd's waits for VectorE: 3.6 and 6.0 by the rows above, where 2.5 and 4.1 were entered. The tail (14.8 against 14.6) was right. loose then showed the term's inside: without the rings round 0 takes 89.8, where it took 91.3 before the change.

**The rivals.** "The rings don't bite" was priced at 1994 without any wait of GpSimd, whose add_terms 13 would have ended 61.5 us after the block's start (2.0 and 59.5); in loose it ended at 74.8, with 9.7 us of waits for VectorE and 3.1 for ScalarE ahead of it, and the real kernels without rings are at 2004 to 2007. The mutual exclusion of VectorE and GpSimd is there, but did not decide. Of the six shifts, three were long: 0.99 at 653.85, 0.99 at 729.47 and 1.21 at 753.21, against 0.14 at 745.81. Two of these are shown, each with GpSimd's instruction beside it, and the short one:

```profile
729.40 1.04 POOL L1458 TENSOR_TENSOR e_kv_raw<-e_ke 128x512 f32<-128x512 f32 x1
729.47 0.99 DVE L2347 SCALAR_TENSOR_TENSOR e_pshift<-e_pmv,e_prstd 128x1 f32<-128x1 f32 x1 [0.87 <-POOL e_prstd L1490]
753.15 1.26 POOL L1442 TENSOR_TENSOR e_dn_lo<-e_dn_raw,e_dn_hi 128x512 fp32r<-128x512 f32 x1
753.21 1.21 DVE L2347 SCALAR_TENSOR_TENSOR e_pshift<-e_pmv,e_prstd 128x1 f32<-128x1 f32 x1 [0.66 <-POOL e_prstd L1490]
745.81 0.14 DVE L2347 SCALAR_TENSOR_TENSOR e_pshift<-e_pmv,e_prstd 128x1 f32<-128x1 f32 x1
```

The long shifts end with GpSimd's instruction, at 730.46 and 730.44, 754.42 and 754.41; at 745.81 GpSimd stood idle (745.08 to 747.40). In these rows a shift takes what is left of the instruction that it meets. All six take 3.9 us and the two cuts 1.5, together 5.4 in place of the 18.7 of the rival's price.

**The sum.** 2023.0 against 2023.26 is better than the steps were. -2.0 of stores, -1.8 of turns and -0.9 of the boundary that were not in it stand against +2.5 of round 0, and the two profiled executions lie 1.7 over and 1.1 under their medians. That it fits to 0.3 us is luck, with executions of the changed kernel from 2020.2 to 2025.2.

## What to carry to other kernels

Walk a new order through all engines, list by list, with each wait in the code: in the chain of the slowest engine, each step that stood behind an unrelated read on ScalarE cost about 6 us here (18.0 in three rings), and reading the lists found it before any run did. Then ask at once for the order without it. A slow transfer's price is not only its end but also the loads behind it, so look for late loads after every issue of the same kind. And price a stall from start to start of the instructions around it, not by the idle time in its row (1.67 against 1.90 here).

## What the runs showed of the hardware

Three things came unexpected. A DMA pattern of 4 x 4 pieces whose steps fit together ran as one of 16 (medians 2024.07 and 2024.23, a wait of 2.7 us at the end in both). Nearly the same idle time of TensorE, 2.1 to 2.2 us at 641 us of the same kernel, was followed by a granted clock of 0.62 in one execution and 1.00 in others; behind the late load of the last round it was 1.00 after 1.7 us of waiting (before), 0.57 after 1.9 (turns_only) and 0.59 after 2.5 (store_old). And four of VectorE's six shifts in round 0 ended within 0.02 us of the GpSimd instruction that ran beside them.
